# The last, short key tile of an attention: 64 keys laid twice for two value products instead of three, and one key left to VectorE

## The reference

```
kvx = einsum('bsi,oi->bso', cond, w_kv_x)          # cond: 8 x 1601 x 512
kx, vx = split(kvx, 2)                              # 8 groups of 128
kx = _ln(kx, kxln_w, kxln_b)
scores = einsum('bsghd,btgd->bghst', qx, kx) / sqrt(128)
p = softmax(scores, axis=-1)                        # over t = 0 .. 1600
xout = einsum('bghst,btgd->bsghd', p, vx)
```

## Time and profile before

| | |
|---|---|
| median of 3 runs | 1958.88 us (1955.85 to 1959.55) |
| the profiled execution | 1954.86 us, span 1953.5 us |
| PE busy | 1885.1 us (96%) |
| DVE busy | 1116.1 us (57%) |
| ACT busy | 954.9 us (49%) |
| POOL busy | 629.9 us (32%) |
| DMA | 280.67 MB, mean 144 GB/s |

### The profile page before, as it was taken

The page is one execution under the profiler, slowest core; times in us unless marked ns, Lnnn a source line. Parts: engine busy times, 40 slices in busy tenths (PEclk is TensorE's granted clock), DMA queues, the critical chain, the costliest instruction groups (busy, mean ns, idle before and its releaser), DMA issues.

```text
span 1953.5 us, 30912 instructions
## 1 busy us (share of the span) xinstructions
PE 1885.1 (96%) x10129; PEld 1601.4 (82%) x10129; DVE 1116.1 (57%) x2969; ACT 954.9 (49%) x1956; POOL 629.9 (32%) x742
## 2 busy tenths in 40 slices
PE   6899999999999999999999999999999999999879
PEld 5778888888888888888888888888888888875357
DVE  7765565645564556456655665566556654546853
ACT  5654454545554556445544554455445544435611
POOL 4335543322232223333333333343333332201010
PEclk9999999999999999999999999999999999999979
DMA  7674354535453455335443544354435432475020
GB/s 271 227 248 142 113 158 129 160 113 158 141 175 113 136 157 172 110 104 180 133 149 111 174 133 142 113 175 148 141 113 179 153 113 81 153 242 175 4 86 22
DMA packets 220208, 280.67 MB, mean 144 GB/s; under 512 B 60873, under 2 KB 123594, under 8 KB 220050
## 3 DMA queue, kind: packets, MB, share of 16 engines
q1 hardware_dynamic: 209410, 277.73, 45.1%
q10 hardware_dynamic: 8592, 0.54, 0.3%
q0 software_dynamic: 2048, 0.43, 0.1%
HBM read 238.85 MB, written 39.22 MB: 142 GB/s over the span
## 4 chain that ended last, share of the span: by engine, by line
PE 70%; DVE 5%; issue 5%; POOL 5%; DMA 4%; ACT 3%; SPq 1%; ACTq 0%; POOLq 0%; DVEq 0%
PE u_ps L614 8%; PE u_ps L615 7%; PE u_ps L616 7%; PE kx_ps L510 7%; PE kx_ps L508 7%; PE kx_ps L512 7%; PE t_ps L599 4%; PE sc_ps L585 2%; DMA stage<-in_ctx_n 2%; PE sc_ps L586 2%; PE sc_ps L587 2%; PE ssq_ps L527 2%; PE t_ps L640 2%; PE t_ps L623 1%; POOL rstd_col L1288 1%
## 5 line engine op out<-in xcount | busy, mean ns | idle before, releaser
L508 PE MATMUL kx_ps<-ctxT_hi,wk_hi 128*128 128x400 f32 (+1 forms) x1024 | 363.9, 355 | 5.9 <-DVE ctxT_lo L290 5.6
L510 PE MATMUL kx_ps<-ctxT_lo,wk_hi 128*128 128x400 f32 (+1 forms) x1024 | 355.3, 347 | 0.0
L512 PE MATMUL kx_ps<-ctxT_hi,wk_lo 128*128 128x400 f32 (+1 forms) x1024 | 354.0, 346 | 0.0
L614 PE MATMUL u_ps<-ctxN_hi,pt_hi 128*128 128x512 f32 (+1 forms) x832 | 341.2, 410 | 5.2 <-DVE pt_lo L838 5.2
L615 PE MATMUL u_ps<-ctxN_lo,pt_hi 128*128 128x512 f32 (+1 forms) x832 | 329.9, 397 | 0.0
L616 PE MATMUL u_ps<-ctxN_hi,pt_lo 128*128 128x512 f32 (+1 forms) x832 | 328.5, 395 | 0.0
L838 DVE TENSOR_TENSOR pt_lo<-t_ps,pt_hi 128x512 fp32r<-128x512 f32 (+1 forms) x256 | 144.4, 586 | 248.2 <-ACT pt_hi L1088 248.2
L1057 ACT ACTIVATE kx_hi<-kx_ps 128x400 fp32r<-128x400 f32 (+1 forms) x256 | 129.0, 504 | 304.0 <-PE kx_ps L512 302.4
L1088 ACT ACTIVATE pt_hi<-t_ps 128x512 fp32r<-128x512 f32 (+1 forms) x256 | 125.6, 522 | 260.1 <-PE t_ps L599 260.0
L765 DVE TENSOR_TENSOR kx_lo<-kx_ps,kx_hi 128x400 fp32r<-128x400 f32 (+1 forms) x256 | 146.6, 573 | 175.3 <-ACT sq L1059 174.5
L820 DVE CUSTOM_DVE_ANT_0 prob<-sc_ps,rstd_bc 128x400 f32<-128x400 f32 (+2 forms) x256 | 136.4, 570 | 140.4 <-PE sc_ps L587 140.4
(11 more groups left out here) (282 smaller groups left out, 3497.6 us busy)
## 6 DMA issues: line engine op xcount, KB each, us to landing
rstd_bc<-scratch_rstd SPq DMA_DIRECT2D x64, 804.0 KB, 6.0
stage<-in_ctx_t SPq DMA_DIRECT2D x96, 267.0 KB, 4.4
stage<-in_ctx_n SPq DMA_DIRECT2D x96, 256.0 KB, 6.3
wk_hi<-scratch_wk_s SPq DMA_DIRECT2D x56, 256.0 KB, 3.1
wk_lo<-scratch_wk_s SPq DMA_DIRECT2D x56, 256.0 KB, 3.3
wv_hi<-scratch_wv_s SPq DMA_DIRECT2D x56, 256.0 KB, 4.8
wv_lo<-scratch_wv_s SPq DMA_DIRECT2D x56, 256.0 KB, 5.6
scratch_own_rows<-out_sb SPq DMA_DIRECT2D x32, 256.0 KB, 2.7
```

The source lines that it names most:

```text
L508: PE.matmul(kx_ps[:, j % 2, 0:w], wk_hi[:, g % 2, i, :], ctxT_hi[:, i, c0:c0 + w], start=(i == 0), stop=False)
L510: PE.matmul(kx_ps[:, j % 2, 0:w], wk_hi[:, g % 2, i, :], ctxT_lo[:, i, c0:c0 + w], start=False, stop=False)
L512: mm = PE.matmul(kx_ps[:, j % 2, 0:w], wk_lo[:, g % 2, i, :], ctxT_hi[:, i, c0:c0 + w], start=False, stop=(i == C - 1))
L614: PE.matmul(u_ps[:], pt_hi[0:w, t % 2, cols], ctxN_hi[0:w, y, :], start=(y == 0), stop=False)
```

## The change

The 1601st key leaves the last tile, which keeps 64 keys. The host lays the context rows 1536 to 1599 twice (`ctx_n` now has 1664 rows), and VectorE copies the 64 probabilities beside themselves, so that `turn_prob(n, 3)` transposes a full tile of 128 with each key in two rows. `ctxN_hi[:, 12]` holds the high parts in rows 0 to 63 and the rests in rows 64 to 127; one matmul then gives hi x hi and hi x lo together, and only lo x hi (64 rows) follows. Of the 65-row tile's three matmuls two are left; the transposed block grows from 65 to 128 columns.

The 1601st key's share is added elsewhere. Its context row is loaded once per batch, broadcast over the 128 partitions (`load_last`, a DMA on SP). VectorE makes inv_sum, then `p_last = prob[1600] * inv_sum`, then the copy of the 64 probabilities (`inverse`, now behind prob_low(n+1, 1)). GpSimd writes `u_sb = ctx_last * p_last` (`weigh_last`, at the head of its iteration), and VectorE evicts `u_sb = u_ps * inv_sum + u_sb` (`values_out`), which ScalarE did before. The small statistics tiles are joined in `soft` and `q_small`, and some semaphores are joined.

```diff
         t = k - T0
-        rows = P if t < self.NT - 1 else self.LAST
-        return (dram["ctx_n"][whose, t * P:t * P + rows, :], self.stage[0:rows, k % self.RING, 0:self.E],
-                self.ctxN_hi[0:rows, t, :], self.ctxN_lo[0:rows, t, :])
+        lo = self.ctxN_lo[:, t, :] if t < self.NT - 1 else self.ctxN_hi[self.LAST:P, t, :]
+        return (dram["ctx_n"][whose, t * P:t * P + P, :], self.stage[:, k % self.RING, 0:self.E],
+                self.ctxN_hi[:, t, :], lo)
...
+    def load_last(self, b):
+
+        SP = self.core.SP
+        after(SP, self.last_weighed, self.G * b)
+        SP.dma_start(self.ctx_last[:], self.core.dram["ctx_last"][b, :].partition_broadcast(P)).then_inc(self.last_in, 16)
...
+                if t == NG - 1:
+                    PE.wait_ge(inv_done, 3 * n + 3)
                 for k, y in enumerate(tiles(t)):
-                    w = P if y < NT - 1 else LAST
-                    mm = PE.transpose(t_ps[0:w, t % 2, k * P:(k + 1) * P], prob[:, y * P:y * P + w], ident[:])
+                    mm = PE.transpose(t_ps[:, t % 2, k * P:(k + 1) * P], prob[:, y * P:(y + 1) * P], ident[:])
...
-                    PE.matmul(u_ps[:], pt_hi[0:w, t % 2, cols], ctxN_hi[0:w, y, :], start=(y == 0), stop=False)
-                    PE.matmul(u_ps[:], pt_hi[0:w, t % 2, cols], ctxN_lo[0:w, y, :], start=False, stop=False)
+                    cols, w = slice(k * P, (k + 1) * P), P if y < NT - 1 else LAST
+                    PE.matmul(u_ps[:], pt_hi[:, t % 2, cols], ctxN_hi[:, y, :], start=(y == 0), stop=False)
+                    if y < NT - 1:
+                        PE.matmul(u_ps[:], pt_hi[:, t % 2, cols], ctxN_lo[:, y, :], start=False, stop=False)
                     mm = PE.matmul(u_ps[:], pt_lo[0:w, t % 2, cols], ctxN_hi[0:w, y, :], start=False, stop=(y == NT - 1))
...
+            def inverse(n):
+
+                V.wait_ge(exp_done, n + 1)
+                after(V, u_moved, n)
+                V.reciprocal(inv_sum[:], row_sum[:]).then_inc(inv_done, 1)
+                V.wait_ge(inv_done, 3 * n + 1)
+                after(V, x.last_weighed, n)
+                V.tensor_tensor(p_last[:], prob[:, SK - 1:SK], inv_sum[:], ALU.mult).then_inc(inv_done, 1)
+                V.wait_ge(inv_done, 3 * n + 2)
+                V.tensor_copy(prob[:, SK - 1:SK - 1 + LAST], prob[:, SK - 1 - LAST:SK - 1]).then_inc(inv_done, 1)
+
+            def values_out(n):
+                V.wait_ge(u_done, NG * (n + 1))
+                V.wait_ge(x.last_weighed, n + 1)
+                V.scalar_tensor_tensor(u_sb[:], u_ps[:], inv_sum[:], u_sb[:], ALU.mult, ALU.add).then_inc(u_moved, 1)
...
                 refill(1)
+                if v and s:
+                    query_low(n + 1)
+                    if r:
+                        query_stats(n + 2)
                 if v:
-                    V.wait_ge(exp_done, n + 1)
-                    after(V, u_moved, n)
-                    V.reciprocal(inv_sum[:], row_sum[:]).then_inc(inv_done, 1)
+                    values_out(n)
                 if s:
-                    if v:
-                        query_low(n + 1)
-                        if r:
-                            query_stats(n + 2)
                     scale_scores(n + 1, 0)
                     scale_scores(n + 1, 1)
...
                     prob_low(n + 1, 0)
                     prob_low(n + 1, 1)
+                    inverse(n + 1)
...
-                    A.wait_ge(inv_done, n + 1)
-                    A.wait_ge(u_done, NG * (n + 1))
-                    after(A, ut_turned, n)
-                    A.activation(u_sb[:], u_ps[:], ACTF.Copy, scale=inv_sum[:, 0:1]).then_inc(u_moved, 1)
...
+            def weigh_last(n):
+
+                G.wait_ge(inv_done, 3 * n + 2)
+                if n % G_ == 0:
+                    G.wait_ge(x.last_in, 16 * (n // G_ + 1))
+                after(G, ut_turned, n)
+                G.tensor_scalar(u_sb[:], x.ctx_last[:], p_last[:], None, ALU.mult).then_inc(x.last_weighed, 1)
...
+                if n >= 0:
+                    weigh_last(n)
                 if 0 <= n and n + 1 < N:
                     query_high(n + 1)
...
+                if g == G_ - 1 and n + 1 < N:
+                    x.load_last(b + 1)
                 refill(5, 6, 7)
```

More of the change, by code:

```diff
@@ L221, in __init__ @@
         dram, sem = core.dram, core.stage_sem
-        self.B, self.SK, self.E = dram["ctx_n"].shape
+        self.B, self.E = dram["ctx_last"].shape
         self.KP = dram["ctx_t"].shape[3]
+        self.SK = self.KP - 1
         self.G = dram["wk_s"].shape[1]
@@ L226, in __init__ @@
         self.NT = -(-self.SK // P)
-        self.LAST = self.SK - (self.NT - 1) * P
+        self.LAST = self.SK - 1 - (self.NT - 1) * P
         self.NG = -(-self.NT // 4)
@@ L252, in place_values @@
         self.ctxN_hi = self.core.sb(stack, "ctxN_hi", [P, self.NT, self.E], F32R)
-        self.ctxN_lo = self.core.sb(stack, "ctxN_lo", [P, self.NT, self.E], F32R)
+        self.ctxN_lo = self.core.sb(stack, "ctxN_lo", [P, self.NT - 1, self.E], F32R)
+        self.ctx_last = self.core.sb(stack, "ctx_last", [P, self.E])
     def piece(self, whose, k):
@@ L382, in attend @@
         ctxN_hi, ctxN_lo = x.ctxN_hi, x.ctxN_lo
[L383 to L386, removed]
+        prob = sb("prob", [P, NT * P])
+        soft = sb("soft", [P, 10])
+        chunk_max, row_max, neg_bias, exp_bias = soft[:, 0:4], soft[:, 4:5], soft[:, 5:6], soft[:, 6:7]
+        row_sum, inv_sum, p_last = soft[:, 7:8], soft[:, 8:9], soft[:, 9:10]
         pt_hi, pt_lo = sb("pt_hi", [P, 2, 512], F32R), sb("pt_lo", [P, 2, 512], F32R)
@@ L522, in key_squares @@
                     u, odd = divmod(n - 3, 2)
[L523 removed]
+                    PE.wait_ge(own_less, 2 * u + 2)
                     if odd:
@@ L784, in query_stats @@
                 V.wait_ge(q_in[m % 2], 32 * (m // 2 + 1))
-                V.bn_stats(q_st[:], q_nat[:, m % 2, :]).then_inc(q_stat, 1)
-                V.wait_ge(q_stat, m + 1)
+                V.bn_stats(q_st[:], q_nat[:, m % 2, :]).then_inc(q_mvd, 1)
+                V.wait_ge(q_mvd, 2 * m + 1)
                 after(V, q_normed, m)
@@ L852, in own_less_maximum @@
                 V.wait_ge(own_scored, u + 1)
-                V.tensor_reduce(own_mx[:], s3, AX.X, ALU.max).then_inc(own_maxed, 1)
-                V.wait_ge(own_maxed, u + 1)
+                V.tensor_reduce(own_mx[:], s3, AX.X, ALU.max).then_inc(own_less, 1)
+                V.wait_ge(own_less, 2 * u + 1)
                 after(V, own_p_turned, u)
@@ L1084, in prob_high @@
                 d = NG * n + t
-                rows, cols = (P, 512) if t < NG - 1 else (LAST, P)
+                cols = 512 if t < NG - 1 else P
                 A.wait_ge(pt_turned, d + 1)
                 after(A, u_done, d - 1)
-                A.activation(pt_hi[0:rows, t % 2, 0:cols], t_ps[0:rows, t % 2, 0:cols], ACTF.Copy).then_inc(pt_high, 1)
+                A.activation(pt_hi[:, t % 2, 0:cols], t_ps[:, t % 2, 0:cols], ACTF.Copy).then_inc(pt_high, 1)
             def own_queries(u):
@@ L1204, in scalar @@
                     A.wait_ge(bias_set, n + 2)
-                    after(A, inv_done, n + 1)
+                    after(A, inv_done, 3 * n + 3)
                     A.activation(prob[:, 0:SK], prob[:, 0:SK], ACTF.Exp, bias=exp_bias[:, 0:1], scale=SCALE,
@@ L1251, in query_norm @@
             def query_norm(m):
-                G.wait_ge(q_mvd, m + 1)
+                G.wait_ge(q_mvd, 2 * m + 2)
                 after(G, q_rsd, m)
@@ L2286 @@
         "ctx_t": ctx_t,
-        "ctx_n": ctx,
+        "ctx_n": ctx[:, np.r_[0:SK - 1, SK - 65:SK - 1], :],
+        "ctx_last": ctx[:, SK - 1, :],
         "consts": np.concatenate([column(parts[n]) for n in COLS] + [np.tile(row_parts[n].reshape(1, -1), (P, 1)) for n in ROWS
```

16 lines of the change are left out of this document (9 added, 7 removed).

## The result

The changed kernel took 1967.44 us (median of 6 runs, 1961.95 to 1969.31), the kernel before beside it 1956.88 (1953.95 to 1959.55, 6 runs). The ratio is 1.0055, 95% interval 1.0044 to 1.0066: 10.6 us **slower**, where I had forecast 6.9 us faster (1952.0 against 1958.88). It is also outside my range. The profiled execution took 1969.31 us.

A forecast was written before the change was run, and what follows sets the result against it. TensorE, busy for all 24.00 of 24 us, was taken to bound the kernel. The terms -15.0 + 2.0 + 0.7 + 0.4 + 5.0 gave -6.9 us, from the median of 1958.88 to 1952.0 us, range 1945.5 to 1958.5.

The forecast's parts named there:

- Part 1: Last tile's removed product on TensorE: 64 matmuls at a step of 0.235 us each, 15.0 us won.
- Part 2: Refill units: 13 keep only 0.08 us of 0.235, 2.0 us taken back; unit 13, pt_lo delayed by inverse, 0.7 us.
- Part 3: Eviction moved to VectorE: scale_scores up to 0.1 us late in 18 odd units, 0.4 us lost (0 to 1.8).
- Part 4: New broadcast DMA of ctx_last delays the critical context piece at 7 batch boundaries: 5.0 us lost (4.0 to 9.0).
- Blocking by weigh_last: Rival, 13%: GpSimd's weigh_last holds VectorE for 1.33 us where context pieces precede pt_lo; +6.6 us, 1965.5 us.
- Eviction as the bound: Rival, 5%: values_out on VectorE ends too late in every unit, giving the product back; about +8 us.
- Broadcast hidden: Rival, 27%: the last row's load at batch boundaries costs nothing; -11.9 us, 1947.0 us.

The follow-up runs named there:

- full_rows: Changed kernel with the last tile's low product (pt_lo) on all 128 rows instead of 64, made by prob_low: 1948.84 us, ratio 0.9965 to the kernel before.
- before_64: Kernel before, with only the last of the last tile's three products on 64 rows instead of 65: 1976.42 us, ratio 1.0104.
- twice_64: Changed kernel with the low product of the last tile but one on 64 rows too: 1987.64 us, ratio 1.0158 to the kernel before.
- full_once: full_rows with the last context row loaded once only, ahead of unit -1's other loads: 1944.91 us, ratio 0.9945 to the kernel before.
- no_last: full_rows without load_last, weigh_last, p_last and values_out; eviction back on ScalarE, reciprocal back ahead of q_lo, probability copy kept: 1942.30 us, ratio 0.9932 to the kernel before.
- full_early: full_rows with each batch's last-row load issued at the head of SP's iteration, not right ahead of the last context pieces: 1945.05 us, ratio 0.9944 to the kernel before.
- late_inverse: full_early with inverse behind refill(7) and keys_low on VectorE, and weigh_last behind query_high on GpSimd: 1943.76 us, ratio 0.9942 to the kernel before.

## Why the prediction was wrong

**Part 1 failed**, at the sentence "A matmul of 65 rows has the same step, so 64 products removed are 64 x 0.235 = 15.0 us of a gapless TensorE queue". The price of the removed product was right: full_rows gained 8.2 / 33 = 0.25 us per plain unit. What I didn't price is the product that stays, which goes from 65 rows to 64. I read the earlier trace rows as "rows don't matter"; it shows only that 65 don't. The term lacking is 64 switches in and 64 out, 0.385 us in a plain unit and less where TensorE waits, 17.6 to 20 us in all by three comparisons (full_rows against the changed kernel, before_64, twice_64).

The Trainium skill has a rule for this ("TensorEngine Tiling (Array Packing)", section "Key Properties"): a change of the tiling mode, not of the tile alone, drains TensorE; by its section "Available Configurations" the modes have 128, 64 or 32 rows. The trace agrees as far as it can: 65 rows run like 128, 64 don't, and two 64-row products in a row pay once. No row names a mode, though, so that it is the mode's change which costs is the page's word. The measured price is 0.19 us a switch. With that price on 64 pairs, 24.6 us, my sum would have been +17.7: too much, but with the right sign.

**Part 2** (+2.0 and +0.7) was right in kind. Refill units kept nothing of the removed product, -0.1 us in 14 units of full_rows, where my terms give -0.5. The 0.08 us of the reciprocal's slot can be read off: nine of the 14 are shorter by 0.05 to 0.09 us in full_once, and all but unit 21 are within 0.01 us of the kernel before in no_last, which has the reciprocal ahead of q_lo again. Unit 13 waited for pt_lo for 0.17 us in the earlier trace rows, 0.68 in the kernel after, 0.57 in full_rows and 0.29 in full_early, and not at all in late_inverse and no_last. So the wait is there only with `inverse` ahead of the pieces, but it cost the unit 0.15 us in full_rows, not 0.5. Units 5, 23 and 29 lost 0.3, 0.1 and 0.2 us as well, which I hadn't seen coming. In no_last they lose nothing, so it is the added operations; late_inverse clears unit 5 alone, and which operation holds up unit 29 stays open.

**Part 3** (+0.4) was about right: full_once, with all the added operations and no load per batch, differs by 0.2 us in 33 plain units from no_last, which has none of them but the copy of the probabilities. The timeline of an odd unit after, where the earlier trace rows had ScalarE:

```profile
1048.97 0.75 DVE L870 SCALAR_TENSOR_TENSOR u_sb<-u_ps,soft,u_sb 128x512 f32<-128x512 f32 x1 [2.18 <-PE u_ps L631]
1049.85 0.58 DVE L835 CUSTOM_DVE_ANT_0 prob<-sc_ps,rstd_bc 128x402 f32<-128x402 f32 x1
...
1050.06 0.47 PEld L638 LDWEIGHTS t_ps<-consts,u_sb 128*128 128x128 f32 x4
```

0.75 us (I said 0.73), ended at 1049.72, and the transposes load from 1050.06. weigh_last took 1.57 us, as the 1.56 of t_below in the earlier trace rows said. As a whole the added work cost little: full_once 0.9945 and no_last 0.9932, within each other's intervals, and all the periods in the table but unit 0 sum to 0.1 us between the two.

**Part 4** (+5.0, 4.0 to 9.0) was right in its mechanism: the broadcast isn't hidden, and it delays the critical piece at boundary 16 by 0.8 us. That the sum at the boundaries came out at 4.8 us is partly luck, since 1.5 of it is the clock, which I had no term for; 3.3 is the delay, and the medians say 3.9 for both. The sign that I named, TensorE waiting for pt_lo 0.7 to 0.9 us longer than before at boundaries 16 to 48, came at boundary 32 alone: the waits were 1.35, 1.43, 0.22, 0.90 and 0.59 us before and 1.89, 1.95, 0.96, 0.76 and 0.55 after. Without the load (full_once) only 1.09 and 1.07 are left, at 16 and 24. So the load adds 0.55 to 0.96 us, but the rest of the change had shortened these waits first. That gain wasn't in my sum: the seven boundaries won 3.0 us in full_once and 2.9 in no_last, for 7 x 0.235 = 1.6. What makes it stays open.

**The rivals.** Blocking by weigh_last: of seven pairs of `low` operations that ran beside it in refill units six took 1.33 us for two, as ever, and one 1.75. Eviction as the bound: no, as full_once against no_last shows. Broadcast hidden: no. Of all I wrote, only the last clause, that the product's step might not be freed by something "that the windows don't show", points to what happened, and I gave it no price and no chance. Put right by the one term, the sum is good: -6.9 forecast for what full_rows does, -8.1 measured. Part of that is misses that cancel: by the periods of full_rows the plain units won 8.2 us for 7.4 by my terms, the refill units 0.1 for 0.5, and the boundaries lost 1.8 for 3.4.

Unit 0 is not the change's: its period was 2.2 us longer in the second profile of the unchanged kernel too, and 2.0 to 4.9 in all others. So the first profile was short there, and the span against which the sum was made with it.

## What to carry to other kernels

Before a matmul gets fewer rows, look at which side of 64 it lands on, compared with its neighbours (64, 65 and 128 rows were measured here): one product of 64 rows between products of 128 costs more (0.385 us) than the whole product that was saved (0.235). Filling the rows up to 65 or 128 costs nothing; here the 64 spare rows even carried the low-times-low share. And a new DMA for later use goes where the queue is quiet, not ahead of the piece that the chain waits for: the same 256 KB cost 4 us at one place and, by the medians, nothing measurable at another.
